# Summing a dot product over three components with one reduction instead of two additions, on the vector engine

## The chip, the cores and the metric

The kernel runs on one core of a Trainium2 chip. The metric is the device time of one execution in microseconds (us). The kernel before takes 1456.11 us, the median of three runs (1455.35, 1456.11, 1456.16). A measured difference of under 0.2% (2.9 us) is not told from no change here.

## The reference, cut to what matters

The program is a chain of four graph layers over 1250 nodes with 512 features and 40,000 edges. The change lies in the third layer, an equivariant message layer. For each edge it takes a scalar part `s` and a vector part `v` (32 channels with three components each) of the node that the edge comes from, and combines them with the edge's direction `yv` (three components):

```python
s = hs[idx_j]
v = hv[idx_j]                       # (edges, 32, 3)
ys = Yr_ij[:, 0]
yv = Yr_ij[:, 1:4]
t_s1 = s * ys[:, None]
t_s2 = jnp.einsum('efc,ec->ef', v, yv) * IS3      # the dot product
t_v1 = s[:, :, None] * yv[:, None, :]
t_v2 = v * ys[:, None, None]
...
edge = concat([t_s1 * Wf[..., 0], t_s2 * Wf[..., 1], t_v1 * Wf[..., 2:3], t_v2 * Wf[..., 3:4], ...])
agg = jax.ops.segment_sum(edge, idx_i, num_segments=n)
```

Only these four of the reference's terms reach the output; the kernel computes no other. `t_s2` is what the change touches: for each edge and channel, the sum over three components of `v * yv`.

## The kernel before, in words

Edges are handled in chunks of 128, one edge to a partition. A step of the message stage takes four chunks (`QUAD`), and there are 81 steps (`STEPS`). The first eight steps and the last one are written out, and the 72 between run in a loop whose body holds eight steps. A step has these parts:

- GpSimd (POOL, `gather_dst`, L930) issues three indirect DMAs of 128 rows of `u`, the nodes' projected features (32 scalar values, then 3 x 32 vector values). The first of the four chunks of a step needs no gather: its rows come from a product on TensorE that ScalarE copies into the ring (L1187 and L723, for four steps at a time). The ring holds eight steps, and before gathering step st POOL waits until VectorE has finished step st - 8 (`after(pool, m_ok, used)`).
- TensorE (PE) multiplies the radial features of the step by `w2_blk` (L1195, L1197), and ScalarE (ACT, L732) scales part of the product into `py`. Both wait until VectorE has finished the step two before the one they work for.
- VectorE (DVE, function `messages`) waits for the gathered rows (`u_in`), then runs nine operations in program order: `vy`, the products of `u`'s three vector components and the direction (L1906, 384 elements a partition); `hot`, the one-hot matrix of the edge's other node (L1908, 512); the first addition into `v_sum` (L1911, 128); a 384-element message part that needs `py` (L1913, behind a wait on `p_ok`); the second addition into `v_sum` (L1916, 128); `sw` (L1917), another message part (L1918) and the product with `v_sum` (L1920), 128 elements each; and the last message part (L1922, 384). The last one raises `m_ok`.
- TensorE then adds the step's messages into the accumulators in PSUM, by products of `hot` and `msg` (L1221, two records for each of the four chunks).

`vy` lies in memory as (chunk, component, channel), so that the three values that are added together are 32 elements (128 bytes) apart. An operation that reads what an earlier one on the same engine wrote waits for the semaphore `v_ok`, which four operations of a step raise.

Once in four steps DVE also prepares the next four: `hid` (L1930, 512 elements) and three small ones (L1937, L1941, L1943); PE and ACT have matching pieces (L1180, L1187, L1206, L1212; L716, L723, L738). SyncE (SP) loads the sorted attributes of four steps at a time, 256 KB each. It waits for POOL (`at_free`), PE and DVE (`y_ok`) of an earlier lap. When it has issued the last of these loads it issues the loads of the next layer's weights.

After step 80 PE closes the accumulators, and the rest of the program (the end of the third layer and the fourth) depends on them.

Of the kernel before, what the change touches and what calls it, by code (L numbers as in the profile page):

```python
# [91 lines left out]
def graph_layers(nc, src, dst, dst_next, etype, norm, attr, x, bases, w_comp, h_bias, g_w1, g_b1, g_w2, g_b2,  # L92
# [5 lines left out]
    ALU, ACT = mybir.AluOpType, mybir.ActivationFunctionType  # L98
# [8 lines left out]
    with ctx:  # L107
        def sb(scope, name, shape, dt):
            return scope.enter_context(nc.sbuf_tensor(name, shape, dt))
# [117 lines left out]
        vy = sb(late, "vy", [P, QUAD, 3, HID], f32)  # L227
        v_sum = sb(late, "v_sum", [P, QUAD, HID], f32)
# [55 lines left out]
        def semaphores(names):  # L284
            return [sem(n) for n in names.split()]
# [36 lines left out]
        u_pe, u_ev, t_pe, t_act, h_pe, h_act, h_ok, w_pe, y_ok, p_ok, v_ok, m_ok, m_pe, agg_ok, pre_ok = semaphores(  # L322
            "u_pe u_ev t_pe t_act h_pe h_act h_ok w_pe y_ok p_ok v_ok m_ok m_pe agg_ok pre_ok")
# [73 lines left out]
        def u_ring(st):  # L397

            return u_first if isinstance(st, int) and st < RING else u
# [22 lines left out]
        def lap_u(st, s, columns):  # L422

            return 2 * columns * (st - s) + 16 * columns
# [6 lines left out]
        def after(eng, s, value):  # L431

            if not isinstance(value, int) or value > 0:
                eng.wait_ge(s, value)
# [941 lines left out]
        def _(dve):  # L1376
            v = nc.vector
# [391 lines left out]
            def layers(graph, near):  # L1769
# [123 lines left out]
                def messages(st, r, par, s8):  # L1893
                    first = 0 if near else 1
                    us = u_ring(st)[:, s8, first:first + QUAD, 0:HID]
                    uv = u_ring(st)[:, s8, first:first + QUAD, HID:P].rearrange("p c (y f) -> p c y f", y=3)
                    out_v = msg[:, par, :, 2 * HID:MSG].rearrange("p c (y f) -> p c y f", y=3)
                    w = ps[par][:, :].rearrange("p (c w) -> p c w", c=QUAD)
                    rpar, q = s8 // QUAD % 2, s8 % QUAD * QUAD
                    y = yr[:, rpar, q:q + QUAD, 1:4].unsqueeze(3).broadcast_to([P, QUAD, 3, HID])  # L1900
                    dve.wait_ge(y_ok, r + 1)
                    after(dve, m_ok, st)
                    if near:
                        dve.wait_ge(near_ev, 2 * (r + 1))
                    dve.wait_ge(u_in[s8], lap_u(st, s8, QUAD - 1 if near else QUAD))
                    v.tensor_tensor(vy[:, :, :, :], uv, y, ALU.mult).then_inc(v_ok, 1)  # L1906
                    after(dve, m_pe, st - 1)
                    v.tensor_tensor(hot[:, par, :, :], iota_h[:, :].unsqueeze(1).broadcast_to([P, QUAD, P]),  # L1908
                                    src_of[:, rpar, q:q + QUAD, :].broadcast_to([P, QUAD, P]), ALU.is_equal)
                    dve.wait_ge(v_ok, st * 4 + 1)  # L1910
                    v.tensor_tensor(v_sum[:, :, :], vy[:, :, 0, :], vy[:, :, 1, :], ALU.add).then_inc(v_ok, 1)  # L1911
                    dve.wait_ge(p_ok, st + 1)
                    v.tensor_tensor(out_v[:, :, :, HID:2 * HID],  # L1913
                                    py[:, par, :, HID:2 * HID].unsqueeze(2).broadcast_to([P, QUAD, 3, HID]), uv, ALU.mult)
                    dve.wait_ge(v_ok, st * 4 + 2)
                    v.tensor_tensor(v_sum[:, :, :], v_sum[:, :, :], vy[:, :, 2, :], ALU.add).then_inc(v_ok, 1)  # L1916
                    v.tensor_tensor(sw[:, :, :], w[:, :, 3 * HID:P], us, ALU.mult).then_inc(v_ok, 1)  # L1917
                    v.tensor_tensor(msg[:, par, :, 0:HID], py[:, par, :, 0:HID], us, ALU.mult)  # L1918
                    dve.wait_ge(v_ok, st * 4 + 3)
                    v.tensor_tensor(msg[:, par, :, HID:2 * HID], w[:, :, 2 * HID:3 * HID], v_sum[:, :, :], ALU.mult)  # L1920
                    dve.wait_ge(v_ok, st * 4 + 4)
                    v.tensor_tensor(out_v[:, :, :, 0:HID], sw[:, :, :].unsqueeze(2).broadcast_to([P, QUAD, 3, HID]), y,  # L1922
                                    ALU.mult).then_inc(m_ok, 1)

                def message(st, r, par, s8):
                    rpar = (s8 // QUAD + 1) % 2
                    if more(r + 1) and s8 % QUAD == 3:
                        dve.wait_ge(h_act, r + 2)
                        after(dve, w_pe, st - QUAD + 1)
                        v.scalar_tensor_tensor(hid[:, rpar, :], soft[:, 0, :], -LOG2, soft[:, 1, :],  # L1930
                                               ALU.add, ALU.add).then_inc(h_ok, 1)
                    if valid(st):
                        messages(st, r, par, s8)
                    if more(r + 1) and s8 % QUAD == 0:
                        dve.wait_ge(ld_at[rpar], loaded(r + 1, rpar))
                        after(dve, near_pe, 2 * (r + 1) - 1)
                        v.tensor_copy(dst_b[:, :, :], at[:, rpar, :, 0, DSTC:DSTC + 1].bitcast(i32))  # L1937
                        if not isinstance(r, int) or r >= 1:
                            dve.wait_ge(m_ok, st)
                            dve.wait_ge(p_ok, st)  # L1940
                        v.tensor_scalar(src_of[:, rpar, :, :], slot_words(rpar, SRCC, SRCC + 1).bitcast(i32), P - 1, None,  # L1941
                                        ALU.bitwise_and)
                        v.tensor_tensor(yr[:, rpar, :, :], slot_words(rpar, YCOL, YCOL + 4),  # L1943
                                        slot_words(rpar, RCUT, RCUT + 1).broadcast_to([P, QUAD * QUAD, 4]), ALU.mult)\
                            .then_inc(y_ok, 1)
# [196 lines left out]
```

## Time and profile before

| | |
|---|---|
| profiled execution, its own time | 1456.16 us |
| its span | 1454.3 us |
| busy over the span: PE, weight loads, DVE, ACT, POOL | 94%, 64%, 59%, 34%, 61% |
| message stage: first product `vy` to the last message part | 873.5 to 1183.2 us |
| first and last gather of the stage issued | 856.4 and 1174.2 us |

The span is what lies between the first and the last instruction. The 1.9 us around it belong to the execution and not to a stage. The busy shares are averages over stages of very different kinds: in the message stage PE, DVE and POOL are all busy most of the time, so which of them sets the pace must be read from what each waits for. A row of a timeline gives the start and the duration of an instruction. Two VectorE instructions in a row overlap, so what one takes of the engine's time is the distance between its start and the next one's start, called its pitch here, and not its duration.

### The profile page before, as it was taken

Reading aid. Unit: us, or ns where it says so; the run is one execution under the profiler, and the core shown is the slowest. Engines: PE = TensorE matmul, PEld = TensorE weight load, DVE = VectorE, ACT = ScalarE, POOL = GpSimd, SP = SyncE. Lnnn points to the kernel's source line nnn. Section 1 sums busy time; section 2 is a strip of 40 time slices with the busy share of each in tenths; the row PEclk is TensorE's granted clock in tenths of the full one; section 3 lists DMA queues with packets and bytes.
Section 4 is the critical chain, followed back from the end, with each engine's and each line's share of the span. In section 5 each row is a group of like instructions: output and inputs, shape, how many; then the busy total and the mean of one; then the engine's idle time right before and its main releaser. Section 6 shows DMA issues by size and latency. Waiting matters only on the chain. (4 is left out here: it accounts for less than half of the span.)

```text
span 1454.3 us, 24122 instructions
## 1 busy us (share of the span) xinstructions
PE 1364.6 (94%) x6924; PEld 937.1 (64%) x6925; DVE 861.3 (59%) x2485; ACT 494.5 (34%) x1279; POOL 892.1 (61%) x927
## 2 busy tenths in 40 slices
PE   4888799999999999999999989998999979999998
PEld 2778788888885444444694866665666656686565
DVE  8778755555554667776433429988888854411111
ACT  7000000000005888882521235654555546311100
POOL 5777777777777777777777767777777720000000
PEclk9999999999999999999999989999999989999999
DMA  4678789888885652233211122222222330000000
GB/s 164 193 228 232 237 288 312 259 239 257 269 263 159 171 163 83 76 84 110 57 26 26 37 60 59 71 65 64 74 67 65 87 77 1 30 0 30 8 29 35
DMA packets 104166, 172.96 MB, mean 119 GB/s; under 512 B 20155, under 2 KB 54128, under 8 KB 104080
## 3 DMA queue, kind: packets, MB, share of 16 engines
q0 software_dynamic: 42832, 103.15, 24.2%
q10 hardware_dynamic: 27790, 39.30, 8.8%
q1 hardware_dynamic: 33458, 29.39, 6.5%
q8 instruction: 50, 0.82, 0.2%
q14 instruction: 36, 0.29, 0.1%
HBM read 153.74 MB, written 18.02 MB: 118 GB/s over the span
## 5 line engine op out<-in xcount | busy, mean ns | idle before, releaser
L874 POOL DMA_INDIRECT gath<-h_rows,idx x313 | 303.0, 968 | 95.0 <-issue 66.8
L1008 PEld LDWEIGHTS ps<-spread,gath 128*128 128x128 f32 x2504 | 306.9, 197 | 73.8 <-issue 43.4
L1008 PE MATMUL ps<-spread,gath 128*128 128x96 f32 x2504 | 313.0, 281 | 24.6 <-DMA gath<-h_rows,idx 17.7
L1030 PE MATMUL ps<-base_t,z 128*128 128x512 f32 (+1 forms) x640 | 308.4, 603 | 0.0
L930 POOL DMA_INDIRECT u<-u_rows,at x219 | 218.6, 998 | 66.8 <-issue 63.4
L1550 DVE TENSOR_TENSOR z<-z,ps 128x384 f32 x313 | 172.7, 552 | 100.1 <-PE ps L1008 88.5
L900 POOL DMA_INDIRECT slots<-att,idx_s x160 | 161.6, 1010 | 49.5 <-issue 47.6
L1221 PE MATMUL ps<-msg,hot 128*128 128x256 f32 x648 | 162.4, 394 | 20.6 <-DVE msg L1922 19.5
L900 POOL DMA_INDIRECT slots<-z,idx_s x153 | 153.5, 1003 | 43.9 <-issue 41.2
L1221 PEld LDWEIGHTS ps<-msg,hot 128*128 128x128 f32 x648 | 119.2, 192 | 81.0 <-DVE msg L1922 59.8
L1030 PEld LDWEIGHTS ps<-base_t,z 128*128 128x128 f32 (+1 forms) x640 | 107.3, 188 | 75.1 <-issue 74.9
L613 ACT ACTIVATE z<-ps 128x512 f32<-128x512 f32 x5 | 3.0, 597 | 408.6 <-PE ps L1030 408.6
L621 ACT ACTIVATE hot_s<-iota_a,src_i 128x128 f16<-128x128 f16 x314 | 107.4, 389 | 31.7 <-PE ps L1326 26.2
L732 ACT ACTIVATE py<-ps,yr 128x64 f32<-128x64 f32 x324 | 75.0, 314 | 104.8 <-PE ps L1197 97.5
L1732 DVE TENSOR_TENSOR cnt<-cnt,ps 128x120 f32 x313 | 87.8, 281 | 31.1 <-DVE cnt L1732 2.5
L1090 PE MATMUL ps<-wa,ht 128*128 128x512 f32 (+1 forms) x240 | 104.8, 592 | 0.0
L1115 PE MATMUL ps<-adj,hs 128*128 128x384 f32 (+3 forms) x240 | 88.5, 369 | 0.0
L1115 PE MATMUL ps<-adj,hl 128*128 128x384 f32 (+3 forms) x240 | 84.6, 352 | 0.0
L1102 PE MATMUL ps<-hs,adj 128*128 128x512 f32 (+1 forms) x200 | 83.9, 420 | 0.0
L1197 PE MATMUL ps<-w_blk,hid 128*128 128x512 f32 x162 | 83.8, 599 | 0.0
L1102 PE MATMUL ps<-hl,adj 128*128 128x512 f32 (+1 forms) x200 | 78.7, 394 | 0.0
L1090 PEld LDWEIGHTS ps<-wa,ht 128*128 128x128 f32 (+1 forms) x240 | 44.3, 188 | 53.2 <-issue 53.1
(297 smaller groups left out, 1837.8 us busy)
## 6 DMA issues: line engine op xcount, KB each, us to landing
base_t<-in_bases_dram ACTq DMA_DIRECT2D x116, 256.0 KB
slots<-att SPq DMA_DIRECT2D x21, 256.0 KB, 5.2
at<-slots SPq DMA_DIRECT2D x21, 256.0 KB, 2.7
gath<-h_rows,idx POOLq DMA_INDIRECT x313, 4.2
u<-u_rows,at POOLq DMA_INDIRECT x219, 2.5
att<-in_attr_dram SPq DMA_DIRECT2D x40, 64.0 KB
slots<-att,idx_s POOLq DMA_INDIRECT x160
z<-in_attr_dram SPq DMA_DIRECT2D x39, 64.0 KB
```

Of the source, the lines that this page charges most:

```text
L621: last = nc.scalar.activation(hot_s[:, p % PAIRS, c, :], iota_a[:, 0:P], ACT.Abs, bias=src_neg[:, 2 * p + c:2 * p + c + 1])
L874: nc.gpsimd.indirect_dma_start(out=gath[:, c % RING, :], out_offset=None, in_=h_rows, in_offset=bass.IndirectOffsetOnAxis(ap=idx[:, par, c ...
L900: nc.gpsimd.indirect_dma_start(out=slots, out_offset=bass.IndirectOffsetOnAxis(ap=idx_s[0:r, turn_of, c:c + 1], axis=0), in_=att_of[slot][ ...
L930: nc.gpsimd.indirect_dma_start(out=u_ring(st)[:, s8, c + 1 - skip, :], out_offset=None, in_=u_soon if soon else u_rows, in_offset=bass.Ind ...
L1008: last = mm(bank[:, k * SPREAD:(k + 1) * SPREAD], gath[:, h_slot, k * P:(k + 1) * P], s_of.rearrange("p b d -> p (b d)"), start=True, stop ...
L1030: return mm(ps[BANKS[n]][0:rows(n), :], z[:, k, b, n * P:n * P + rows(n)], base_t[:, k, :], start=(t == JOINS[n]), stop=(t == JOINS[n] + T ...
L1090: last = mm(ps[6 + p % 2][0:r, :], ht[:, k, n * P:n * P + r], w[k], start=(k == 0), stop=(k == KIN - 1))
L1102: last = mm(bank[0:r, :], graph[0:rows(s), s, n * P:n * P + r], part[0:rows(s), s, :], start=(i == 0 and part is upper), stop=(i == BLOCKS ...
L1115: last = mm(bank[:, 0:b - a], part[0:rows(s), s, k * P:(k + 1) * P], graph[0:rows(s), s, a:b], start=(j == 0 and part is upper), stop=(j = ...
L1221: last = mm(acc[:, bass.ds(place[c], MSG)], hot[:, par, c, :], msg[:, par, c, :], start=False, stop=False)
L1550: v.tensor_tensor(zw, zw, bank[:, 0:KIN * SPREAD].rearrange("p (k b d) -> p k b d", k=KIN, b=BASES), ALU.add)\
L1732: v.tensor_tensor(cw, cw, ps[5 + t // QUAD % 2 * 2][:, q % QUAD * AWIN:(q % QUAD + 1) * AWIN] .rearrange("p (d s) -> p s d", s=BLOCKS), AL ...
```

## The change

The two additions are replaced by one `tensor_reduce` over the innermost axis of a view of `vy` in which the component comes last. It stands where the first addition stood. One of the two waits between the parts of the sum goes, and the count of `v_ok` is three a step in place of four.

```diff
-                    dve.wait_ge(v_ok, st * 4 + 1)
-                    v.tensor_tensor(v_sum[:, :, :], vy[:, :, 0, :], vy[:, :, 1, :], ALU.add).then_inc(v_ok, 1)
+                    dve.wait_ge(v_ok, st * 3 + 1)
+                    v.tensor_reduce(v_sum[:, :, :], vy[:, :, :, :].rearrange("p c y f -> p c f y"), mybir.AxisListType.X, ALU.add)\
+                        .then_inc(v_ok, 1)
                     dve.wait_ge(p_ok, st + 1)
                     v.tensor_tensor(out_v[:, :, :, HID:2 * HID],
                                     py[:, par, :, HID:2 * HID].unsqueeze(2).broadcast_to([P, QUAD, 3, HID]), uv, ALU.mult)
-                    dve.wait_ge(v_ok, st * 4 + 2)
-                    v.tensor_tensor(v_sum[:, :, :], v_sum[:, :, :], vy[:, :, 2, :], ALU.add).then_inc(v_ok, 1)
                     v.tensor_tensor(sw[:, :, :], w[:, :, 3 * HID:P], us, ALU.mult).then_inc(v_ok, 1)
                     v.tensor_tensor(msg[:, par, :, 0:HID], py[:, par, :, 0:HID], us, ALU.mult)
-                    dve.wait_ge(v_ok, st * 4 + 3)
+                    dve.wait_ge(v_ok, st * 3 + 2)
                     v.tensor_tensor(msg[:, par, :, HID:2 * HID], w[:, :, 2 * HID:3 * HID], v_sum[:, :, :], ALU.mult)
-                    dve.wait_ge(v_ok, st * 4 + 4)
+                    dve.wait_ge(v_ok, st * 3 + 3)
```

## Rows read from the trace of the kernel before

**Rows 1.** Busy time by stretch: PE, weight loads, DVE, ACT, POOL; clock, DMA share, GB/s.

```profile
877.00:937.00 60.00, 59.52 (x283) 41.30 (x282) 57.21 (x175) 35.22 (x103) 47.20 (x43) 1.00 0.20 59
937.00:1164.00 227.00, 211.94 (x978) 140.45 (x976) 196.70 (x588) 123.67 (x357) 173.03 (x178) 0.99 0.24 72
1164.00:1184.00 20.00, 14.90 (x63) 10.46 (x64) 13.66 (x41) 8.15 (x23) 8.69 (x9) 0.91 0.55 129
```

**Rows 2.** Waits, 877 to 1184 us: waiter, releaser, total us, times, longest us.

```profile
POOL u L930 <- issue: 63.4, 208, 0.3
...
DVE vy L1906 <- DMA u<-u_rows,at: 33.5, 50, 4.0
...
POOL u_first L930 <- DVE msg L1922: 0.6, 2, 0.3
```

**Rows 3.** Timeline of POOL in the middle of the stage.

```profile
1100.30 0.94 POOL L930 DMA_INDIRECT u<-u_rows,at  x1 [0.30 <-issue]
1101.55 0.97 POOL L930 DMA_INDIRECT u<-u_rows,at  x1 [0.30 <-issue]
```

**Rows 4.** Timeline of DVE, first steps and catching up with the gathers.

```profile
877.95 0.55 DVE L1906 TENSOR_TENSOR vy<-u_first,yr 128x384 f32<-128x384 f32 x1
...
933.47 0.55 DVE L1906 TENSOR_TENSOR vy<-u,yr 128x384 f32<-128x384 f32 x1
...
937.98 0.56 DVE L1906 TENSOR_TENSOR vy<-u,yr 128x384 f32<-128x384 f32 x1 [1.42 <-DMA u<-u_rows,at]
```

**Rows 5.** Timeline of POOL: last gathers of steps 1 and 17.

```profile
862.71 0.95 POOL L930 DMA_INDIRECT u_first<-u_soon,at  x1 [0.30 <-issue]
...
930.40 1.14 POOL L930 DMA_INDIRECT u<-u_rows,at  x1 [0.30 <-issue]
```

**Rows 6.** Timeline of DVE, step 60 and the start of step 61.

```profile
1101.42 0.28 DVE L1911 TENSOR_TENSOR v_sum<-vy 128x128 f32<-128x128 f32 x1
1101.62 0.54 DVE L1913 TENSOR_TENSOR msg<-py,u 128x384 f32<-128x384 f32 x1
1102.09 0.28 DVE L1916 TENSOR_TENSOR v_sum<-v_sum,vy 128x128 f32<-128x128 f32 x1
1102.29 0.28 DVE L1917 TENSOR_TENSOR sw<-ps,u 128x128 f32<-128x128 f32 x1
...
1104.07 0.59 DVE L1906 TENSOR_TENSOR vy<-u,yr 128x384 f32<-128x384 f32 x1 [0.30 <-DMA u<-u_rows,at]
```

**Rows 7.** Groups by line, DVE: busy us, mean ns of one, idle before.

```profile
L1451 DVE TENSOR_REDUCE inside<-gath 128x1 f32<-128x320 f32 x1 | 0.5, 486 | 0.0
...
L2014 DVE SCALAR_TENSOR_TENSOR xs<-ps,xs 128x128 f32<-128x128 f32 (+1 forms) x10 | 2.9, 286 | 1.9 <-PE ps L1281 1.9
...
L2017 DVE SCALAR_TENSOR_TENSOR xs<-ps,xs 128x384 f32<-128x384 f32 (+1 forms) x10 | 6.8, 682 | 0.0
```

**Rows 8.** Timeline of DVE near the start: the longest reduction.

```profile
31.34 1.13 DVE L1509 TENSOR_REDUCE near_n<-gath 128x10 f32<-128x940 bf16 x1
32.39 0.37 DVE L1510 TENSOR_REDUCE near_n<-gath 128x1 f32<-128x215 bf16 x1
```

**Rows 9.** Timeline of DVE at the stage's end, steps 77 and 79.

```profile
1168.69 0.56 DVE L1906 TENSOR_TENSOR vy<-u,yr 128x384 f32<-128x384 f32 x1 [4.03 <-DMA u<-u_rows,at]
...
1177.81 0.56 DVE L1913 TENSOR_TENSOR msg<-py,u 128x384 f32<-128x384 f32 x1 [0.96 <-ACT py L732]
```

**Rows 10.** The chain that ended last, from its beginning: start, us, what.

```profile
1171.84 3.09 PE ps L1221 x8
...
1178.54 0.68 PE ps L1187 x12
1179.22 0.02 issue
1179.24 0.61 ACT u L723
...
1183.20 1.99 PE ps L1221 x8
```

**Rows 11.** The page's costliest groups: busy us, mean ns, idle before, releaser.

```profile
L930 POOL DMA_INDIRECT u<-u_rows,at x219 | 218.6, 998 | 66.8 <-issue 63.4
```

## The prediction

> **What bounds the kernel now.** The change touches DVE in the message stage alone, so I read the stage by itself. The busy times by stretch [rows 1] show three engines that are nearly full: from 937 to 1164 us PE is busy 211.9 of 227 us, DVE 196.7 and POOL 173.0. Busy time does not decide among them, so I went to the waits. POOL, the least busy of the three, is the one that waits for nobody: 63.4 us of its idle time in 208 pieces of at most 0.3 us are put down to its own issue, and only 0.6 us, in ordinary 0.3 us gaps, to DVE [rows 2]. Its timeline is even: a gather every 1101.55 - 1100.30 = 1.25 us [rows 3], so a step of three gathers takes at least 3.75 us. DVE, on the other hand, sat for 33.5 us in 50 pieces waiting for the rows that these gathers bring [rows 2]. In the middle of the stage POOL sets the pace, then, and DVE follows it.
>
> The stage has three parts. (a) At its beginning POOL is ahead. DVE starts step 1 at 877.95 [rows 4], 15.2 us after the last gather of that step was issued at 862.71 [rows 5]. Sixteen steps later, at 933.47 and 930.40, the distance is down to 3.1 us. DVE is its own bound here, at (933.47 - 877.95) / 16 = 3.47 us a step, and is busy 57.2 of 60 us [rows 1]. At 937.98, step 18, it waits for a gather, 1.42 us [rows 4]. (b) From there to step 76 it follows POOL. (c) Step 77 waits 4.03 us for its rows [rows 9], in a stretch in which the DMA share is 0.55 against 0.24 before [rows 1]; behind it the gathers of steps 78 to 80 are in, and DVE, PE and ACT run on each other. The chain that ended last begins here, with PE's message products of step 77 at 1171.84, then ACT's copy at 1179.24 and step 80 on DVE, which ends in PE's last products at 1183.20 [rows 10].
>
> **The change, part by part.** Removed from DVE's time: the additions. Each lasts 0.28 us, but the next operation starts earlier: 1101.62 - 1101.42 = 0.20 us after the first addition and 1102.29 - 1102.09 = 0.20 us after the second [rows 6]. Together they hold the engine for 0.40 us a step, and not 0.56. The wait that goes with the second one cost nothing: it starts 0.47 us after the 384-element operation in front of it [rows 6], which is that one's ordinary pitch (the first addition finished long before). Over 81 steps 32.4 us of DVE time are removed.
>
> Added: a reduction that reads 384 elements a partition and writes 128. No row has a reduction into so many short groups, so its cost is bounded.
> - Nearest row: 320 float32 elements into one take 486 ns [rows 7]. The row of 940 elements into ten has 1.13 us and a pitch of 32.39 - 31.34 = 1.05 us [rows 8]. From the two, an element costs (1130 - 486) / (940 - 320) = 1.04 ns, and a reduction of 384 takes 486 + 64 x 1.04 = 553 ns. Less the same 0.08 us of overlap (1.13 - 1.05) that is a pitch of 0.47 us, the pitch of the 384-element product at 1101.62. I take this: it is the input that a reduction pays for in both rows.
> - Upper end: the view steps 128 bytes from one element to the next and closes 128 groups. For the stride, an operation that writes every third element takes 682 ns at 384 elements and its neighbour 286 at 128 [rows 7]; 256 more elements at 1.04 ns make 552, so some 0.13 us are the stride's. If closing a group cost one element's time, that is 128 x 1.04 = 0.13 us more. Pitch 0.47 + 0.26 = 0.73 us.
> - Lower end: if the reduction paid for its 128 outputs, it would cost one addition, 0.20 us.
>
> So a step of DVE gets 0.47 - 0.40 = 0.07 us longer (from -0.20 to +0.33): the change saves an instruction, but it makes the engine read each product once at one element a time, which is 384 elements, where the additions took 256 element times. Over 81 steps 5.7 us of DVE time are added.
>
> The Trainium skill, "VectorE: DVE Perf Modes", under "The DRAIN you can't avoid", says that the next operation does not start until the pipe has emptied, and advises keeping the number of operations small. By that the exchange would be two full durations, 0.57 us, for one of 0.55, a gain of 0.02 us a step, and of 1.2 us over the stage if all of it showed. The trace disagrees: starts lie 0.20 us apart where durations are 0.28 [rows 6].
>
> Where these 0.07 us lie:
> - (a) Steps 0 to 17 end 18 x 0.07 = 1.3 us later. Nobody waits for that: DVE's wait of 1.42 us at step 18 shrinks to about 0.2. POOL needs DVE eight steps behind it, and it was never more than 15.2 us, some four steps, ahead. PE's and ACT's work for the following step has a whole DVE step of 3.5 us to be done in.
> - (b) Four steps of POOL take at least 15.0 us. DVE's idle time over these steps is 33.5 us less the 4.03 at step 77, 29.5 us in 59 steps, or 0.50 a step. 0.07 of it is used. Cost 0. If the cover were gone, it would be 59 x 0.07 = 4.1 us.
> - (c) Step 77 starts with its rows at 1168.69, wherever DVE has been before. Its last message part is 0.07 us later, and so are PE's products that open the chain. PE is then busy until 1179.22 [rows 10], so the lateness of step 78 does not show; in step 79 the 0.96 us wait for `py` [rows 9] stands behind the reduction and takes it up, and the second addition's 0.20 us behind that wait is gone. Step 80 starts on ACT's copy and is on the chain to its end: 0.07 us more. Sum for the tail: 0.14 us.
>
> The semaphore's new count costs nothing: the reduction waits for `vy` with `hot` between them, as the addition did, and its reader L1920 comes only after three other operations.
>
> Sum: 0 + 0 + 0.14 = +0.1 us on the profiled execution's own 1456.16, which is 0.05 above the median of the runs. Forecast 1456.3. With the bounds, two steps of the chain give -0.4 to +0.7, 1455.8 to 1456.9; three runs of before spread over 0.8 us, so the forecast's own range is 1455.3 to 1457.4.
>
> **Rivals.**
> 1. *DVE becomes the bound (slower).* This decides where the added time exceeds the idle: 33.5 us over steps 0 to 76, 0.43 us a step, that is a reduction with a pitch above 0.83 us. If short strided groups ran at two element times per element, the pitch would be 0.47 + 0.40 = 0.87, 0.47 us a step more; 77 x 0.47 = 36.2 less 33.5 leaves 2.7 us, and 2 x 0.47 in the tail make 3.6: 1459.8. For it: no row has groups of three, and before 937 us there is no idle time at all, so a late DVE has only the second part to catch up in. Against: no row shows two element times, and even both surcharges together stay at 0.73, below the point.
> 2. *POOL gets faster (faster).* The gathers average 998 ns [rows 11] where an undisturbed one takes 0.94 to 0.97 [rows 3]; over 219 that is about 10 us of disturbance, on the engine that sets the pace. The additions read two tensors in SBUF, the reduction one. The additions hold DVE for 0.40 of at least 3.75 us a step. DVE has other operations of that kind, so I give the additions up to half as much again as this 11%: if such operations cause the disturbance, 1.6 us go: 1454.7, still inside 0.2%. Against: the gathers at 1100.30 and 1101.55 run beside such operations [rows 3, 6] and neither is slowed. The Trainium skill, "SBUF — State Buffer", says that a DVE operation with two SBUF inputs and a GpSimd operation that reads SBUF exclude each other for a whole instruction; here that would be this 1.6 us gain.
> 3. *The chance stalls of POOL fall elsewhere.* A slow gather near the end of the stage moves everything behind it; that is the spread of a kernel, 1 to 2 us to either side, and not an effect.
>
> **How the numbers follow.** Forecast (hidden, +0.1): 78%. Rival 1: 8%, at 1459 and above. Rival 2: 6%. Rival 3: 8%, half to each side, mostly inside 0.2%. The range runs from rival 2's 1454.7, a little lower for the spread, to 1458.0, which leaves rival 1 out: 1454.4 to 1458.0. Faster by over 0.2% (2.9 us, what this measurement can tell from no change): 3%, since no case names such a gain. Slower: 8%. Same: 89%.
>
> **What would show it.** Right: a reduction of about 0.55 us with the next operation starting 0.47 us after it; steps of DVE in the first stretch at 3.54 us; its waits for the gathers down from 33.5 to about 28 us; POOL still at 1.25 us a gather; the stage's last products within a few tenths of 1183.2. Wrong: a reduction with a pitch above 0.83 us and few waits for gathers left (rival 1), or gathers that average nearer to 950 ns (rival 2). If the pitch is right and the time still moves by more than 3 us, I have missed somebody who waits for DVE.

## The result and the profile after

The changed kernel takes 1460.54 us, the median of 13 runs (1457.32 to 1464.65); the kernel before, run beside it, 1455.14 (1453.61 to 1458.48). The ratio is 1.004 with a 95% interval of 1.003 to 1.005: slower, by some 5 us where 0.1 was forecast, and 2.5 us above the upper end of the predicted range.

The profiled execution after took 1460.38 us, its span is 1458.5 (before: 1454.3). Its groups by line, for DVE and POOL (busy us, mean ns of one, idle before):

```profile
L1911 DVE TENSOR_REDUCE v_sum<-vy 128x128 f32<-128x384 f32 x81 | 47.4, 586 | 0.0
...
L930 POOL DMA_INDIRECT u<-u_rows,at x219 | 224.2, 1024 | 66.7 <-issue 62.2 <-DMA u<-u_rows,at 2.7 <-DVE msg L1921 1.8
```

The reduction takes 586 ns, and the next operation starts 0.50 us after it (1107.80 - 1107.29 below). Against the two additions that is 0.10 us a step more, where 0.07 was estimated. The second line is the surprise: nothing was changed on POOL, and yet its gathers average 1024 ns where they took 998 [rows 11]. 219 times 26 ns are 5.7 us, on the engine that sets the pace. Part of this comes back elsewhere, as the stretches below show.

The waits of the stage (total us, times, longest) show that DVE still has idle time that ends with a gather, 28.3 us against 33.5 [rows 2]. DVE has not become the bound:

```profile
DVE vy L1906 <- DMA u<-u_rows,at: 28.3, 43, 4.0
```

Where POOL lost time is seen when its busy time is cut into stretches (busy us, number of gathers, clock, DMA share, GB/s). First before, then after:

```profile
880.00:960.00 80.00, 62.01 (x60) 1.00 0.22 64
960.00:1160.00 200.00, 152.44 (x157) 0.99 0.23 68
```

```profile
880.00:960.00 80.00, 63.50 (x55) 0.98 0.21 58
960.00:1160.00 200.00, 152.47 (x157) 1.00 0.24 68
```

From 960 us the two kernels issue the same 157 gathers in the same time. From 880 to 960, while DVE catches up with the gathers and runs without a break, POOL gets through 55 where it did 60, each at 1155 ns in place of 1034. Five gathers at 1.25 us are 6 us, but the cut at 880 us flatters the kernel before: its slowest gather of the stage, 2.99 us from 877.79 on, lies across it. That one is of the first eight steps, whose tile is `u_first`, and these took longer before. The lines of `u_first` over 850 to 1190 us, before and after:

```profile
L930 POOL DMA_INDIRECT u_first<-u_rows,at x12 | 14.6, 1217 | 3.7 <-issue 3.0 <-DVE msg L1922 0.6
```

```profile
L930 POOL DMA_INDIRECT u_first<-u_rows,at x12 | 11.7, 972 | 3.7 <-issue 3.0 <-DMA u_first<-u_soon,at 0.3 <-DVE msg L1921 0.3
```

All 243 gathers of the stage took 245.0 us before and 247.2 after, 2.2 us more. The two profiled executions differ by 4.2 us. The first gather was issued 0.8 us later (857.16 against 856.38), the last one 2.7 us later (1176.87 against 1174.16), and the stage's tail behind step 77 took 1.2 us more. So in this pair about half of the loss lies in the gathers' durations.

The timeline of POOL in the catching up, and DVE's beside it, after:

```profile
922.47 1.26 POOL L930 DMA_INDIRECT u<-u_rows,at  x1 [0.30 <-issue]
924.04 2.12 POOL L930 DMA_INDIRECT u<-u_rows,at  x1 [0.30 <-issue]
```

```profile
922.37 0.55 DVE L1914 TENSOR_TENSOR msg<-py,u 128x384 f32<-128x384 f32 x1
...
924.19 0.55 DVE L1906 TENSOR_TENSOR vy<-u,yr 128x384 f32<-128x384 f32 x1
924.66 0.68 DVE L1908 TENSOR_TENSOR hot<-iota_h,src_of 128x512 f32<-128x512 f32 x1
925.26 0.59 DVE L1911 TENSOR_REDUCE v_sum<-vy 128x128 f32<-128x384 f32 x1
```

The gather at 922.47 begins while L1914 runs. L1914 ends at 922.92, and the gather at 923.73, 0.81 us later. The one at 924.04 ends at 926.16, 0.82 us after `hot` (924.66 + 0.68 = 925.34). Both DVE operations read two tensors in SBUF. The one that follows `hot` is the reduction, which reads one. The same picture comes back every 14.0 us (at 910.01, 924.04, 937.90 and 951.93, 2.11 or 2.12 us each time). It is an order, and not chance. The kernel before has such an order too. One gather in every 14 us lasts 1.92 or 1.93 us (at 892.61, 906.51, 920.54 and 934.38). It begins inside `hot`, runs past the first addition and L1913, and ends 0.82 us after the second addition (921.36 + 0.28 = 921.64; 922.46); all four read two tensors in SBUF, and `sw` behind them reads one:

```profile
920.54 1.92 POOL L930 DMA_INDIRECT u<-u_rows,at  x1 [0.30 <-issue]
```

```profile
921.36 0.28 DVE L1916 TENSOR_TENSOR v_sum<-v_sum,vy 128x128 f32<-128x128 f32 x1
921.56 0.28 DVE L1917 TENSOR_TENSOR sw<-ps,u 128x128 f32<-128x128 f32 x1
```

So the longest gathers are not what the change added. It added short delays: from 880 to 960 us 29 gathers last over 1.05 us where 10 did, nine of them 1.26 to 1.28 us behind L1914. Later, in the settled part, a gather begins inside the reduction:

```profile
1107.43 0.94 POOL L930 DMA_INDIRECT u<-u_rows,at  x1 [0.30 <-issue]
```

```profile
1107.29 0.58 DVE L1911 TENSOR_REDUCE v_sum<-vy 128x128 f32<-128x384 f32 x1
1107.80 0.54 DVE L1914 TENSOR_TENSOR msg<-py,u 128x384 f32<-128x384 f32 x1
```

It lasts 0.94 us, undisturbed.

One thing in this trace turned out to be no cause: TensorE still runs at the lower of its two clocks, 1.2 GHz, when the stage starts, and longer here than before. The stretch 875 to 880 us, before and after (PE, weight loads, DVE, ACT, POOL, clock, DMA share, GB/s):

```profile
875.00:880.00 5.00, 5.00 (x22) 3.07 (x21) 4.09 (x15) 2.29 (x9) 4.21 (x3) 0.94 0.26 87
```

```profile
875.00:880.00 5.00, 5.00 (x10) 1.44 (x9) 4.25 (x14) 0.93 (x4) 3.83 (x4) 0.50 0.37 105
```

From 880 to 885 us the granted clock was still 0.61. DVE's steps 1 and 2 took 4.37 and 6.41 us, against 3.18 and 3.88.

### The profile page after: what moved, and what is told of

It is laid out like the page before. It is cut to its first block and busy times, and to the rows that moved or that the text cites. A ratio compares the mean times of both kernels' runs of the same rounds, so it can differ in the third digit from the quotient of the medians.

```text
span 1458.5 us, 23969 instructions
## 1 busy us (share of the span) xinstructions
PE 1368.8 (94%) x6924; PEld 942.1 (65%) x6925; DVE 866.0 (59%) x2404; ACT 494.7 (34%) x1279; POOL 892.9 (61%) x927
## 5 line engine op out<-in xcount | busy, mean ns | idle before, releaser
L1008 PEld LDWEIGHTS ps<-spread,gath 128*128 128x128 f32 x2504 | 310.6, 199 | 72.4 <-issue 43.0
L930 POOL DMA_INDIRECT u<-u_rows,at x219 | 224.2, 1024 | 66.7 <-issue 62.2
L900 POOL DMA_INDIRECT slots<-z,idx_s x153 | 155.5, 1017 | 43.9 <-issue 41.2
L1221 PEld LDWEIGHTS ps<-msg,hot 128*128 128x128 f32 x648 | 119.7, 193 | 82.2 <-DVE msg L1921 61.7
```

Source lines behind the costliest of these rows:

```text
L900: nc.gpsimd.indirect_dma_start(out=slots, out_offset=bass.IndirectOffsetOnAxis(ap=idx_s[0:r, turn_of, c:c + 1], axis=0), in_=att_of[slot][ ...
L930: nc.gpsimd.indirect_dma_start(out=u_ring(st)[:, s8, c + 1 - skip, :], out_offset=None, in_=u_soon if soon else u_rows, in_offset=bass.Ind ...
L1008: last = mm(bank[:, k * SPREAD:(k + 1) * SPREAD], gath[:, h_slot, k * P:(k + 1) * P], s_of.rearrange("p b d -> p (b d)"), start=True, stop ...
L1221: last = mm(acc[:, bass.ds(place[c], MSG)], hot[:, par, c, :], msg[:, par, c, :], start=False, stop=False)
```

## The experiments

Three theories. D: the time goes with DVE's time. P: a gather on POOL waits for a DVE operation with two inputs in SBUF, and the change moves DVE's operations against the gathers. C: the late clock at the stage's start. Each ratio is to the kernel before, run on the same chip.

**e1, the reduction in another place.** The same operations, two of them exchanged:

```diff
-                    (reduction)
                     dve.wait_ge(p_ok, st + 1)
                     v.tensor_tensor(out_v[:, :, :, HID:2 * HID], ...)
+                    (reduction)
```

> The changed kernel with its reduction moved behind the 384-element message part that needs py, where the second addition had stood: the same operations and the same DVE time a step, in another order. Theory D (DVE's added 0.10 us a step costs the time): as the changed kernel, 1460 to 1461. Theory P (the gathers are slowed wherever they meet DVE operations with two inputs in SBUF, so the order of DVE's operations counts): the mean duration of a gather of u differs from the changed kernel's 1024 ns by 10 ns or more, and the time with it, by 219 times the difference. Theory C (TensorE comes out of its half-speed stretch late at the start of the stage): as the changed kernel where its trace shows the half speed until 883 us, 3 us less where it ends at 876.

Measured: 1482.27 us, ratio 1.018 (1.016 to 1.020). The gathers average 1113 ns. 219 times the 89 ns over the changed kernel are 19.5 us, of the 22 by which it is slower. The reduction still takes 587 ns. D and C give 1460 and fall as a full account; only the order was touched. In the settled part POOL and DVE show it at work, POOL first:

```profile
1107.36 0.94 POOL L930 DMA_INDIRECT u<-u_rows,at  x1 [0.30 <-issue]
1108.61 1.23 POOL L930 DMA_INDIRECT u<-u_rows,at  x1 [0.30 <-issue]
1110.15 1.26 POOL L930 DMA_INDIRECT u<-u_rows,at  x1 [0.30 <-issue]
```

```profile
1108.48 0.54 DVE L1911 TENSOR_TENSOR msg<-py,u 128x384 f32<-128x384 f32 x1
1108.94 0.58 DVE L1914 TENSOR_REDUCE v_sum<-vy 128x128 f32<-128x384 f32 x1
...
1110.04 0.54 DVE L1921 TENSOR_TENSOR msg<-sw,yr 128x384 f32<-128x384 f32 x1
```

The second gather of a step starts 0.13 us into the two-input message part, which stands where the reduction stood, and ends 0.82 us after it (1108.48 + 0.54 = 1109.02; 1109.84). The third does the same behind L1921 (1110.58; 1111.41).

**e2, more DVE time and nothing else.** The kernel before with one more line behind `sw`:

```diff
                     v.tensor_tensor(sw[:, :, :], w[:, :, 3 * HID:P], us, ALU.mult).then_inc(v_ok, 1)
+                    v.memset(v_fill[:, 0:HID], 0.0)
```

> The kernel before, both additions kept, and one more operation a step on DVE, a memset of 32 elements with no input (about 0.1 us, what the reduction costs more than the two additions). Theory D: 1460 to 1461, as the changed kernel. Theory P: the phases move too, but the additions with their two inputs stay, so the time need not follow the added 0.1 us; the mean duration of a gather tells it. Theory C: 1455 to 1456, unless the late return of the clock shows in its trace.

Measured: 1454.18 us, 0.9985 (0.9975 to 0.9996), a little faster than without the memset (85 ns each). The gathers average 990 ns. DVE's added time is not what costs.

**e3, TensorE kept busy before the stage,** in the changed kernel:

```diff
+                for _ in range(6):
+                    mm(ps[5], ones_b[:, :], ones_b[:, :].unsqueeze(1).broadcast_to([P, QUAD, P]), start=True, stop=True)
                 message(*at_step(-3))
```

(and the same ahead of and behind the next of these calls).

> The changed kernel with 18 more bf16 products of 512 columns on TensorE (into a free PSUM bank) in its idle stretches just before the message stage. Theory C: the granted clock is 1.0 when the stage's first products run (about 873 us), DVE's steps 1 and 2 take 3.3 and 3.9 us in place of 4.4 and 6.4, and the time falls by 3 to 4 us, to 1456 to 1457. Theory D: unchanged at 1460 to 1461. Theory P: DVE starts the stage less far behind POOL, so fewer gathers are met in the catching up: 1457 to 1459.

Measured: 1461.95 us, 1.0043 (1.0027 to 1.0058), no gain over the changed kernel. The clock is up, though: 1.00 from 870 us on, and steps 1 and 2 take 3.28 and 3.77 us. The steps came as C has them, and the time did not. DVE started less far behind, first waited for a gather at 924.35 us, and the gathers average 1013 ns. Theory C falls. Two other runs say the same: e4 and g3 below had the late clock too (steps 1 and 2 of 4.38 and 6.27 us, and of 4.37 and 6.36) and were faster than the kernel before. But the smaller gain that P gave, 1457 to 1459, is not seen either; D's 1460 to 1461 is nearest here, and it is e2 and g1 that speak against D.

**e4, the same DVE time with one input.** The kernel before with both additions as reductions over groups of one element, which leaves the sum out (the second, not shown, reads component 2):

```diff
-                    v.tensor_tensor(v_sum[:, :, :], vy[:, :, 0, :], vy[:, :, 1, :], ALU.add).then_inc(v_ok, 1)
+                    v.tensor_reduce(v_sum..., vy[:, :, 0, :].unsqueeze(3), mybir.AxisListType.X, ALU.add).then_inc(v_ok, 1)
```

> The kernel before with each addition replaced by a reduction over groups of one element, 128 elements, one input: the same two operations' time on DVE, but none of the two reads two tensors in SBUF (the sum over the components is left out). Theory P: gathers average less than the 998 ns of the kernel before and the time falls by 1 to 3 us, to 1452 to 1454. Theory D and theory C: as the kernel before, 1455 to 1456.

Measured: 1452.51 us, 0.9977 (0.9966 to 0.9988), 3.3 us less. These take 279 ns where the additions took 287 and 282. The gathers average 982 ns, and 219 x 16 ns are 3.5 us. So the second inputs of the two additions had cost that much, which is the mechanism of the prediction's second rival.

**f1, two inputs in the reduction's place,** in the changed kernel:

```diff
-                    v.tensor_reduce(v_sum[:, :, :], vy[:, :, :, :].rearrange("p c y f -> p c f y"), ...)
+                    v.tensor_tensor(v_two[:, :, :, :], vy[:, :, :, :], uv, ALU.add)
```

> The changed kernel with its reduction replaced, in the same place, by an elementwise addition of 384 elements that reads two tensors in SBUF (its result stands in for the sum). On a chip on which the kernel before takes its usual 1455 us. Theory P (a gather waits for a running DVE operation with two inputs in SBUF that started before it, and ends 0.81 us after that one): one gather in three would now last 1.23 us in place of 0.94, 0.29 us a step over some 60 steps are 17 us, less what the settled order moves: 1470 to 1480. Theory D (DVE's time): 1458 to 1459. Theory R (the reduction as such disturbs the gathers): 1455 to 1456.

Measured: 1490.11 us, 1.0233 (1.0214 to 1.0251), with 0.03 us less DVE time a step than the changed kernel. The group of gathers (the code stands one line lower here):

```profile
L931 POOL DMA_INDIRECT u<-u_rows,at x219 | 250.4, 1143 | 66.8 <-issue 59.1
```

This is the mirror of e4 and the strongest of the set: two inputs in place of one, in the same position, cost 30 us. It came out worse than P's 1470 to 1480: the order moves, and in steps 50 to 54, for example, two or three gathers in a row last 1.23 to 1.37 us. R, that a reduction as such disturbs, falls.

**f2 and f3, `sw` ahead of `vy`,** in the changed kernel and in the one before (the wait for `py` moves with it):

```diff
+                    dve.wait_ge(p_ok, st + 1)
+                    v.tensor_tensor(sw[:, :, :], w[:, :, 3 * HID:P], us, ALU.mult).then_inc(v_ok, 1)
                     v.tensor_tensor(vy[:, :, :, :], uv, y, ALU.mult).then_inc(v_ok, 1)
```

> The changed kernel with sw (one input in PSUM) moved to the head of the step, ahead of vy. On a chip with the usual time for the kernel before. Theory P: a gather issued when the rows land finds no operation with two SBUF inputs in its way; the episodes in the settled part go, the catching up stays: 1453 to 1457, mean gather under 1005 ns. Theory D: 1460 to 1461.

> The kernel before with the same move of sw. Theory P: 1453 to 1458, the time following 219 times the difference of the gathers' mean from 998 ns. Theory D: 1455 to 1456.

Measured: 1466.79 us, 1.0068 (1.0052 to 1.0085), and 1470.39, 1.0108 (1.0091 to 1.0125). Both missed. I had taken the earlier wait for free. It is not; f2's waits:

```profile
DVE sw L1907 <- ACT py L732: 35.0, 76, 0.8
```

In f2 DVE waits for ACT in 76 of its 81 steps and catches up with the gathers only at the end, so it never gets to the settled order. The gathers average 1050 and 1054 ns. The time still followed them: 219 x 52 ns and 219 x 56 ns are 11.4 and 12.3 us, and measured are 11.4 and 15.0. But these two edits moved two things at once and prove little on either.

**f4, groups of three in a row,** the changed kernel with `vy` as (chunk, channel, component):

```diff
-        vy = sb(late, "vy", [P, QUAD, 3, HID], f32)
+        vy = sb(late, "vy", [P, QUAD, HID, 3], f32)
```

> The changed kernel with the component innermost in vy. An earlier look showed its reduction at 544 ns (586 with the 128-byte step) and its product vy at 681 ns (562). DVE is busy 0.08 us a step longer than in the changed kernel. Theory D: 6 us more than the changed kernel if DVE's time counts as such, 1466. Theory P: vy, with two SBUF inputs, holds a gather 0.12 us longer whenever it meets one, and all behind it stands 0.12 us later: 1457 to 1470, with the time following the gathers' mean.

Measured: 1462.03 us, 1.004 (1.0027 to 1.0053), gathers 1055 ns. It lies in P's range and below D's 1466, but the medians of the two kernels are only 1.5 us apart, which tells little. The 1055 ns do not go with this median: the profiled execution was the slowest of ten, 1467.08 us. The durations were seen in e8, the same kernel in an earlier set on another chip (in f4's own trace the reduction takes 547 ns and `vy` 693). That set, e5 to e8 with the edits of f1, f2, f3 and f4, ran on a chip on which the kernel before took 2061 us. The ratios there were 0.983, 0.987, 0.995 and 0.989. The two-input operation that costs 2.3% in f1 costs nothing there (e5: 0.983, interval 0.976 to 0.990), although the gathers of e5 average 1121 ns. In e5 POOL waited 59.5 us for DVE's last message part, in e6 82.2, so there POOL did not set the pace, and longer gathers fell into its waits. The expectation of e8 and its durations:

> The changed kernel with vy laid out with the component innermost, so that the product L1906 writes every third element and the reduction reads its 384 elements one after the other. Tells what of the reduction's 586 ns is due to the 128-byte step: if the stride costs the 0.03 us above the predicted 553, it takes 553 ns here; if it is the closing of 128 groups, it stays at 586. Time: theory P gives what the gathers' mean gives; if only the reduction gets shorter by 0.03 us, within 3 us of the changed kernel.

```profile
L1906 DVE TENSOR_TENSOR vy<-u,yr 128x384 f32<-128x384 f32 x73 | 49.7, 681 | 56.3 <-ACT u L723 39.2 <-issue 13.7 <-DVE msg L1921 1.6
L1911 DVE TENSOR_REDUCE v_sum<-vy 128x128 f32<-128x384 f32 x81 | 44.1, 544 | 0.0
```

The reduction takes 544 ns on elements in a row and 586 with the 128-byte step. Closing 128 groups costs nothing that is seen here (553 was the estimate from long groups), and the 42 ns between the two are the step's. Writing every third element costs `vy` 0.12 us.

**g1, the memset of e2 in the changed kernel.**

> The changed kernel with the memset of 32 elements of e2 behind sw, 0.06 us more of DVE time a step. Theory P: where the changed kernel has settled, the two-input operation hid ends 0.14 us after the start of a gather, just where a gather is held or is not; the episodes of slow gathers begin there. With the filler it ends at 0.20, so that one gather in twelve lasts 1.01 us, 1 us in all, and the episodes (some 3 to 4 us) go: 1456 to 1460, under the changed kernel. Theory D: 1461 to 1463.

Measured: 1452.91 us over 12 runs (1449.62 to 1456.37), 0.9983 (0.997 to 0.9997). It beats both kernels and lies under P's range: 7.6 us less than the changed one, by an operation of 85 ns that computes nothing. POOL in the stretches of above:

```profile
880.00:960.00 80.00, 62.32 (x59) 1.00 0.23 65
960.00:1160.00 200.00, 151.86 (x159) 1.00 0.25 74
```

The gain is larger than expected, and it lies elsewhere: two gathers more in the settled part, where all of it was expected, and four more in the catching up, where the round of four DVE steps now meets POOL's in other places.

**g2, `hid` with one input,** in the changed kernel, as a reduction over groups of one.

> The changed kernel with hid, the 512-element operation of every fourth step, as a reduction over groups of one with one input (the rectified part of the softplus is left out of it); the same DVE time. Theory P: it holds no gather, so the episodes of the settled part and a part of the slow gathers of the catching up go: 1454 to 1458, mean gather 1000 to 1012 ns in place of 1024. Theory D: 1460 to 1461.

Measured: 1457.83 us, 1.0016 (1.0003 to 1.003), inside the range. But the gathers average 1017 ns (1000 to 1012 were expected) and the episodes of slow gathers in the settled part stay, at steps 24, 44, 45, 48 and 66. The end of `hid` is not what sets them off, or not alone.

**g3, one input nearly everywhere.** `hid`, `vy` and the two 384-element message parts of the changed kernel as reductions over groups of one:

> The changed kernel with hid, vy and both 384-element message parts as reductions over groups of one, one input each (their products are left out); DVE's time a step is the same or up to 0.1 us more. Of its large operations only hot, yr and one of 128 elements still read two tensors in SBUF. Theory P: gathers average 955 to 975 ns, and the time falls by 11 to 15 us against the changed kernel, to 1445 to 1450. Theory D: 1460 to 1465.

Measured: 1448.45 us, 0.9945 (0.9924 to 0.9966), 12 us less than the changed kernel at the same DVE time, gathers 971 ns. This was the widest test of P, and both time and mean lie in its ranges.

**g4, `sw` directly behind the reduction,** in the changed kernel:

```diff
                     dve.wait_ge(p_ok, st + 1)
+                    v.tensor_tensor(sw[:, :, :], w[:, :, 3 * HID:P], us, ALU.mult).then_inc(v_ok, 1)
                     v.tensor_tensor(out_v[:, :, :, HID:2 * HID], ...)
```

> The changed kernel with sw directly behind the reduction, in front of the 384-element part that needs py: two operations in a row that hold no gather (0.50 + 0.20 us), and every result as in the reference. Theory P: in the settled part the third gather of a step finds a 128-element two-input operation that ends 0.15 us after its start, so some 0.02 us more, and in the catching up a gather meets a two-input operation less often: 1455 to 1461, the time following the gathers' mean. Theory D: 1460 to 1461.

Measured: 1458.00 us, 1.0016 (1.0002 to 1.003), gathers 1002 ns. Better than the changed kernel, no gain over the one before.

**All traces together.** The table has all runs but e5 to e8, and how many of the 243 gathers of the stage began while a DVE operation with two SBUF inputs was running that still had over 0.17 us to go ("held"). In every trace the median of these ended 0.82 us after that operation, and the others lasted 0.94 or 0.95 us in the median. A trace shows one execution, so its own time stands beside the median of the runs:

| kernel | held | mean of `u`'s gathers, ns | all 243 gathers, us | the profiled execution, us | median of the runs, us |
|---|---|---|---|---|---|
| g3 | 30 | 971 | 235.7 | 1450.06 | 1448.45 |
| e4 | 31 | 982 | 240.5 | 1453.05 | 1452.51 |
| e2 | 58 | 990 | 241.0 | 1451.19 | 1454.18 |
| g1 | 48 | 991 | 240.7 | 1451.54 | 1452.91 |
| before | 51 | 998 | 245.0 | 1456.16 | 1455.14 |
| g4 | 70 | 1002 | 243.9 | 1455.09 | 1458.00 |
| e3 | 61 | 1013 | 247.4 | 1459.66 | 1461.95 |
| g2 | 73 | 1017 | 247.0 | 1457.74 | 1457.83 |
| after | 62 | 1024 | 247.2 | 1460.38 | 1460.54 |
| f2 | 94 | 1050 | 253.8 | 1468.13 | 1466.79 |
| f3 | 85 | 1054 | 255.7 | 1469.79 | 1470.39 |
| f4 | 93 | 1055 | 255.0 | 1467.08 | 1462.03 |
| e1 | 153 | 1113 | 268.2 | 1481.08 | 1482.27 |
| f1 | 153 | 1143 | 276.5 | 1489.80 | 1490.11 |

The time of the profiled execution follows the gathers' total: 1456.16 us plus what the total has over 245.0 gives every one of them to within 3.2 us, over a range of 40. This carries the large effects (e1, f1, f2, f3, f4). The change's own 4 to 5 us are hardly more than those 3.2. The count alone does not order the kernels: e2 has almost as many held gathers as the changed kernel and g2 and g4 have more, and all three are faster. It matters how long each is held.

The Trainium skill, "SBUF — State Buffer", section "SBUF: two separate sides", has the rule: VectorE and GpSimd share one pair of ports, an operation of VectorE with two SBUF inputs and a GpSimd operation that reads SBUF exclude each other, and the one that starts first keeps the pair for its whole instruction. The first half agrees with the held gathers of the table. The second, taken the other way round, these traces bear out only for a part of a gather and for other operations. L1914, with two SBUF inputs, starts 0.37 us into the gather of 1107.43 above and takes its usual 0.54 us. But the cast and the TENSOR_SCALAR that prepare the next four steps, one input each and usually 0.16 and 0.17 us, do wait in the kernel before:

```profile
1102.82 0.95 POOL L930 DMA_INDIRECT u<-u_rows,at  x1 [0.30 <-issue]
```

```profile
1103.36 0.40 DVE L1937 CAST dst_b<-at 128x4 bf16<-128x4 int32 x1
```

The cast ends with the gather (1103.76 and 1103.77). So does, in the fourteen traces of the table, every one of the two kinds that starts 0.2 to 0.4 us ahead of a gather's end; those that start earlier in one take their usual time.

## Why the prediction was wrong, by its own steps

- *What bounds the kernel.* Right, and half used. POOL sets the pace, and DVE waits for it before and after. The step that failed is the next one, in (a) and (b): "Nobody waits for that" and "Cost 0". I asked who waits for DVE by a semaphore, and treated a gather as a fixed 1.25 us. The gather's own duration depends on what DVE runs beside it, a dependence without any semaphore: `u`'s gathers rose from 998 to 1024 ns, and all 243 together took 2.2 us more in the profiled pair, of 4.2. The recorded sign for this came true: the pitch was nearly right, the time moved by more than 3 us, and somebody who waits for DVE had been missed.
- *The reduction's cost.* Estimated pitch 0.47 us, measured 0.50; the excess over the additions was 0.10 and not 0.07 us. The stride accounts for it (f4, e8). A small miss that e2 and g1 show to be without consequence: more DVE time made either kernel faster. The Trainium skill's section "The DRAIN you can't avoid" in "VectorE: DVE Perf Modes", which the prediction sets against the trace, also says that a next operation that is not held starts earlier, so the 0.20 us between starts disagree with only one half of it.
- *Part (a).* The 1.3 us were to vanish in the wait of step 18. The catching up lasted until step 22 (1.87 us of wait at 957.14), and not for DVE's pace: four steps took 13.7 to 14.0 us both before and after, although DVE had 0.4 us more to do in them, and the forecast 3.54 us a step was not seen. So "DVE is its own bound here" was a misreading. DVE still had gaps, and the fuller engine is TensorE, busy 59.52 of 60 us in the same row [rows 1] and 41.90 of 42 after (893 to 935 us, the line below). That it sets the pace there is argued from this; no run took work off it. The catching up began further behind by the late clock, and e3 shows that this is not the loss.

```profile
893.00:935.00 42.00, 41.90 (x200) 28.98 (x201) 40.93 (x109) 25.42 (x75) 33.47 (x29) 1.00 0.21 57
```

- *Part (c).* Step 77 waited 4.03 us as before. Step 79 waited 1.71 us for `py` in place of 0.96, behind products of TensorE that took 3.78 in place of 3.09 us at the lower clock; a tail of 12.6 us from `vy` of step 77 to that of step 80, against 11.4. Other runs had 10.4 (g4) to 12.8 (e1), so a difference of 1.2 us between two single traces cannot be told from scatter, though it is a part of the 4.2 us.
- *Rival 1 (DVE becomes the bound).* Did not happen: 28.3 us of waits for gathers were left, as the forecast's 28. The agreement is in part luck: DVE's added time was larger than forecast, and the stage up to step 77 was 2.1 us longer.
- *Rival 2 (POOL gets faster).* Its mechanism is the real one, at twice the size for what it named: two additions without their second input gave 3.3 us (e4) where 1.6 was worked out. I dismissed it on the gathers of step 60, none of which was slow. Those are gathers of the settled part, in which POOL and DVE stand in a fixed order that happens to be a good one; the slow ones lie in the catching up (1034 ns each before, [rows 5] has one of 1.14 us), and I did not look there. And I gave the mechanism one sign only. It counts which gathers meet which operation, and removing operations moves all the others, either way.
- *Rival 3.* The slow gathers were called chance stalls. At least those that come back every 14 us are not.

What stays open. Why the changed kernel's order in the catching up is worse than that of before was read off its trace and not derived beforehand, and I could not have told the sign of e2, g1 or g4 from the model. Some gathers wait past a first two-input operation for the next one or more (the 2.12 us, and the 1.93 us before), where DVE's operation starts within some 0.03 us of the moment at which they would be held; what decides there was not found. Nor was what sets off the episodes in the settled part. And the split of the loss rests on single traces. In this pair the gathers account for 2.2 of 4.2 us: their time over 0.94 us each grew by 5.8 us from 880 to 960 us and fell by 3.1 before 880. The rest lies mainly ahead of the first gather and in the tail, and its cause is not shown. That most of the 5.4 us between the medians came through the gathers is argued from the other kernels. e3, at the same time as the changed kernel, has its slow gathers earlier and again from 970 to 1030.

## What to carry to other kernels

When an engine sets the pace without waiting for anyone, look at what makes its own instructions longer, in the stretch where they are longest, before calling a change on another engine hidden. On this kernel a VectorE operation with two SBUF inputs holds back a gather that begins inside it (the gather ends 0.82 us after it, and at times after the next such operations), and one with one input costs it nothing. So exchanging two-input operations for one-input ones is a gain only if the order that results is also measured. Where two engines run against each other at fixed rates, try a small shift (here 0.06 us a step) before judging an edit: it moved the time by 7.6 us, more than the edit did. And before charging for longer gathers, see whether the engine that issues them sets the pace: where it did not (e5), they cost nothing.

## What had not been expected of the hardware

- A gather on GpSimd that began inside a VectorE operation with two SBUF inputs ended 0.82 us after that operation (the median in every trace of the table); undisturbed it takes 0.94 us. Behind several such operations in a row one lasted up to 2.99 us.
- A cast of four elements on VectorE that began 0.2 to 0.4 us ahead of a gather's end ended with the gather: 0.40 us in place of 0.16. A product or message part with two inputs that began inside a gather was not delayed (0.54 us).
- A reduction of 384 float32 elements into 128 groups of three: 586 ns with 128 bytes between the elements, 544 in a row. An elementwise product that writes every third element: 681 ns against 562.
- TensorE at 1.2 GHz at the start of a stage made two VectorE steps 3.7 us longer together and the kernel no slower (e3 against the changed kernel; e4 and g3 had it and were faster than the kernel before).
